# Expert jobs of 128 rows, with the second matrices of all experts resident in SBUF

## What is computed

```
logits = silu(x @ rw1 + rb1) @ rw2 + rb2          # 8 per token
k_logits, k_index = top_k(logits, 2);  k_prob = softmax(k_logits)
for e in range(8):
    we = sum(where(k_index == e, k_prob, 0))
    h  = silu(x @ w1[e] + b1[e]) @ w2[e] + b2[e]  # 128 -> 512 -> 128
    out += we * h
```

## Time and profile before

| | |
|---|---|
| median of three runs | 684.16 us |
| the profiled execution, its time | 685.29 us |
| its span, first to last instruction | 683.6 us |
| mean granted TensorE clock, share of full | 0.960 |
| attention and router, until the first job's up matmul | about 494 us |
| expert stage, first up to last down | about 494 to 655 us |
| reading back, weighting, residual | about 660 to 683 us |

### The profile page before, as it was taken

How to read it: one execution, slowest core, us unless ns; L and a number is a source line. 1 busy time by engine, 2 the same in 40 slices (tenths; PEclk the granted TensorE clock), 3 DMA queues, 4 the chain that set the end, 5 groups by cost and what they waited for, 6 DMA issues and landing times. The chain is left out here.

```text
span 683.6 us, 17706 instructions
## 1 busy us (share of the span) xinstructions
PE 588.5 (86%) x5108; PEld 439.8 (64%) x5108; DVE 507.1 (74%) x1888; ACT 508.8 (74%) x1578; POOL 423.3 (62%) x543
## 2 busy tenths in 40 slices
PE   5667789999899899899989989978798989999950
PEld 4444556666666566566666656655577979999940
DVE  6788988999999999999999999997565312222127
ACT  4157799999999999999989999998643434444434
POOL 2660655747668687686776966855366765554535
PEclk9777999999999999999999999999999999999975
DMA  5996678778787788778868878874525777565538
GB/s 142 308 230 202 198 235 248 228 235 248 214 245 241 213 252 246 228 219 260 249 208 242 252 213 247 243 236 148 189 82 174 236 234 228 198 217 185 176 97 274
DMA packets 173125, 149.03 MB, mean 218 GB/s; under 512 B 16182, under 2 KB 162642, under 8 KB 173030
## 3 DMA queue, kind: packets, MB, share of 16 engines
q1 hardware_dynamic: 168054, 139.33, 67.9%
q0 software_dynamic: 4544, 8.44, 3.7%
q10 hardware_dynamic: 432, 0.14, 0.1%
HBM read 83.71 MB, written 65.05 MB: 218 GB/s over the span
## 5 line engine op out<-in xcount | busy, mean ns | idle before, releaser
L711 ACT ACTIVATE P<-NS,nmax 128x256 f32<-128x256 f32 x512 | 254.2, 504 | 50.5 <-DVE nmax L1312 49.6
L1312 DVE CUSTOM_DVE_ANT_0 NS<-psS,bias 128x256 f32<-128x256 f32 x512 | 185.2, 417 | 2.3 <-PE psS L950 1.6
L968 PE MATMUL psT<-ident,P 128*128 128x128 f32 x1024 | 140.0, 281 | 8.9 <-ACT PT L722 8.8
L1267 DVE COPY stage<-psDist 128x768 f32<-128x768 f32 x125 | 118.1, 945 | 33.9 <-issue 25.2
L722 ACT ACTIVATE PT<-psT 128x512 f32<-128x512 f32 x256 | 136.4, 586 | 0.0
L968 PEld LDWEIGHTS psT<-ident,P 128*128 128x128 f32 x1024 | 118.2, 145 | 24.0 <-issue 9.8
L778 ACT ACTIVATE F<-psS,b1T 128x256 f32<-128x256 f32 x156 | 65.4, 471 | 86.5 <-PE psS L1061 86.5
L609 POOL DMA_INDIRECT results_d<-y,row_u x78 | 76.0, 974 | 56.7 <-DVE y L1458 40.8
L711 ACT ACTIVATION_READ_ACCUMULATOR P<-NS,nmax 128x1 f32 x512 | 100.3, 196 | 0.0
L950 PE MATMUL psS<-Kst,Qst 32*128 32x256 f32 x512 | 65.9, 336 | 34.7 <-DVE nmax L1312 29.9
L1061 PE MATMUL psS<-xT,w 128*128 128x256 f32 x312 | 80.6, 381 | 0.3 <-DMA w<-in_L_ffn_w_dram 0.3
(11 more groups left out here) (254 smaller groups left out, 1044.2 us busy)
## 6 DMA issues: line engine op xcount, KB each, us to landing
dist_d<-stage SPq DMA_DIRECT2D x128, 384.0 KB, 3.0
bias<-dist_d SPq DMA_DIRECT2D x256, 192.0 KB, 3.3
w<-in_L_ffn_w_dram SPq DMA_DIRECT2D x39, 512.0 KB, 3.7
x<-slots_d SPq DMA_DIRECT2D x39, 129.0 KB, 3.0
y<-results_d SPq DMA_DIRECT2D x16, 256.0 KB, 5.0
dist_d<-zeros SPq DMA_DIRECT2D x1, 2048.0 KB, 14.4
out_dram<-y SPq DMA_DIRECT2D x8, 256.0 KB, 3.2
results_d<-y,row_u POOLq DMA_INDIRECT x78, 3.0
```

The lines of the kernel that those rows point to most:

```text
L711: act.activation(P[:, p % 2, h, q, :], NS[:, p % 2, h, q, :], ACT.Exp, scale=-1.0, bias=nmax[:, p % 2, k:k + 1], accum_out=lsum[:, b % 2, ...
L968: mm = pe.transpose(psT[:, h, S * k + 128 * q:S * k + 128 * q + 128], P[:, p % 2, h, q, 128 * k:128 * k + 128], ident[:])
L1267: dve.tensor_copy(stage[:, p % STAGES, :, :, :], bank[:, :, 0:2 * RW].rearrange("p h (q c) -> p h q c", q=2)).then_inc(dist_out, 1)
L1312: dve.tensor_tensor_reduce(NS[:, p % 2, h, q, :], psS[:, h, S * q:S * q + S], bias[:, p, h, q, :], 1.0, 3e38, ALU.add, ALU.min, nmax[:, p ...
```

## The change

ET is 128, so a job has one tile; JOBS becomes 71 and FULL 41. The second matrices of all eight experts are loaded once, in attention, by eight DMAs on SP's queue (one per batch from batch 2 to 9) into `w2_s`, 16 KB per partition. `load_w` then loads the first matrix alone, 256 KB, into one of DEEP = 5 buffers, and waits for `up` where it waited for `down`. `go_down` takes its moving operand from `w2_s` at an address that depends on the expert's number, so PE needs that number in a register. PE, ACT and DVE load the numbers of four jobs at a time with the new function `of_tiles`; SP still loads one per job. A step of `tiles` is now a whole job: up of job n (four matmuls of 128 columns), the transpose for job n+1, down of job n-2. F has three buffers instead of two, `y` 24 instead of 12 (of half the size). The pads stand before jobs 33 and 37. `take_x` and `take_rows` are now done in every step. The steps that are interleaved with the closing of attention keep their numbers.

```diff
-ET = 256
+ET = 128
-HELD = 12
-DEEP = 4
-PADS = {FULL - 4: range(0, EXP // 2), FULL - 2: range(EXP // 2, EXP)}
+HELD = 24
+DEEP = 5
+PADS = {FULL - 8: range(0, EXP // 2), FULL - 4: range(EXP // 2, EXP)}
-        w = t("w", [128, DEEP, 2, HID])
+        w2_s = t("w2_s", [128, EXP, HID])
+        w1_s = t("w1_s", [128, DEEP, HID])
+        def of_tiles(engine_type, j, which):
+            if j % 4 == 0 or j == FULL:
+                last = min(j - j % 4 + 4, JOBS if j >= FULL else FULL)
+                _, which[j:last] = nc.values_load_multi_w_load_instructions(
+                    expert[0:1, j:last], engines=(engine_type,), min_val=0, max_val=EXP - 1)
+            return which[j]
...
+                    if n == 4 and 2 <= b < 2 + EXP:
+                        sp.dma_start(w2_s[:, b - 2, :], w2[:, b - 2, :]).then_inc(w2_in, 16)
...
             def load_w(j):
                 e = of_tile(sp, j)
-                past(sp, down, j + 1 - DEEP)
-                sp.dma_start(w[:, j % DEEP, :, :],
-                             w12[bass.ds(e, 1)].rearrange("a p s h -> p (a s) h")).then_inc(w_in[j % DEEP], 16)
+                past(sp, up, j + 1 - DEEP)
+                sp.dma_start(w1_s[:, j % DEEP, :],
+                             w1[bass.ds(e, 1)].rearrange("a p h -> p (a h)")).then_inc(w_in[j % DEEP], 16)
...
+            def unit(j):
+                if j == 0 or j == FULL:
+                    act.wait_ge(planned, 1 + j // FULL)
+                e = of_tiles(mybir.EngineType.Activation, j, which)
+                past(act, down, j - 2)
+                act.wait_ge(up, j + 1)
+                for k in range(HK):
+                    i = act.activation(F[:, j % 3, k, :], psH[:, j % 2, ET * k:ET * k + ET], ACT.Silu,
+                                       bias=b1T[:, bass.ds(e, 1), k:k + 1].rearrange("p a k -> p (a k)"))
...
+            def go_up(j):
+                pe.wait_ge(w_in[j % DEEP], arrivals(j))
+                pe.wait_ge(x_taken, j + 1)
+                past(pe, silu, j - 1)
+                past(pe, max_done, 4 * STEPS if j == 0 else 0)
+                for k in range(HK):
+                    mm = pe.matmul(psH[:, j % 2, ET * k:ET * k + ET], w1_s[:, j % DEEP, 128 * k:128 * k + 128],
+                                   xT[:, j % 2, :], start=True, stop=True)
...
+            def go_down(j):
+                if j == 0 or j == FULL:
+                    pe.wait_ge(planned, 1 + j // FULL)
+                past(pe, w2_in, 16 * EXP if j == 0 else 0)
+                e = of_tiles(mybir.EngineType.PE, j, which)
+                pe.wait_ge(silu, j + 1)
+                past(pe, y_rows, j - 1)
+                past(pe, ctx_done, B if j == 1 else 0)
                 for k in range(HK):
+                    mm = pe.matmul(psY[j % 2][:, 0:E], F[:, j % 3, k, :],
+                                   w2_s[:, bass.ds(e, 1), 128 * k:128 * k + 128].rearrange("p a e -> p (a e)"),
+                                   start=(k == 0), stop=(k == HK - 1))
...
             def tiles(first, last):
                 for n in range(first, last):
+                    if n < JOBS:
+                        go_up(n)
+                    if n + 1 < JOBS:
+                        turn_x(n + 1)
+                    if n > 1:
+                        go_down(n - 2)
...
             def take_rows(j):
                 dve.wait_ge(down, j + 1)
-                e = of_tile(dve, j)
+                e = of_tiles(mybir.EngineType.DVE, j, which)
                 past(dve, y_sent[j % HELD], 16 * EK * (j // HELD))
```

More of the change, by code:

```diff
@@ L168, in program @@
         attention(nc, block, sm, planned, x_v, X, ident, modT, mv, rstd, Wq, bq, Wk, bk, Wv, bv, Wo, bo, rel, c, wmod,
-                  ahead, rw1_s, rb1T, rw2_s, rb2T, w12, rows, slot_u, earlier, ones,
+                  ahead, rw1_s, rb1T, rw2_s, rb2T, w1, w2, rows, slot_u, earlier, ones,
                   slots_d, sent, p2, firstrow, expert, fill, filled, b1T, b2, out_v)
@@ L283, in attention @@
         jobno = t("jobno", [128, JOBS])
[L284 to L287, removed]
+        gone = t("gone", [128, MOST_JOBS, EXP])
+        gone_t = t("gone_t", [128, MOST_JOBS, EXP])
+        ex = t("ex", [128, MOST_JOBS])
+        first_f = t("first_f", [128, MOST_JOBS])
         used = t("used", [128, EXP + 1])
@@ L356, in attention @@
         b2_in = sm("b2_in")
+        w2_in = sm("w2_in")
         w_in = [sm(f"w_in{k}") for k in range(DEEP)]
@@ L661, in _ @@
             fill_rows(B - 2)
-            send_results(0, 1)
+            send_results(0, 2)
             send(B - 4)
             send(B - 3)
-            send_results(1, 3)
+            send_results(2, 6)
             fill_rows(B - 1)
@@ L765, in step @@
                     squash(b - 2, p - 6)
[L767 to L779, removed]
+            which = [None] * JOBS
+            def unit(j):
[7 more added lines that the diff above has]
+                                       bias=b1T[:, bass.ds(e, 1), k:k + 1].rearrange("p a k -> p (a k)"))
                 i.then_inc(silu, 1)
             def units(first, last):
-                for n in range(first, last):
-                    unit(n // 2, n % 2)
+                for j in range(first, last):
+                    unit(j)
             def weighted_part(c):
@@ L1048, in turn_x @@
                 past(pe, pt_done, 2 * STEPS if j == 0 else 0)
[L1049 to L1057, removed]
+                pe.transpose(psX[:, 0:128], x[:, j % DEEP, 0, 0:E], ident[:])\
+                    .then_inc(x_turned, 1)
@@ L1076, in tiles @@
+                mm.then_inc(down, 1)
             def tiles(first, last):
                 for n in range(first, last):
[L1078 to L1084, removed]
+                    if n < JOBS:
[4 more added lines that the diff above has]
+                        go_down(n - 2)
@@ L1139, in _ @@
             pe.matmul(psM[:, 0:EXP], ones[:], total[:], start=True, stop=True).then_inc(counted, 1)
-            tiles(11, 2 * GATES)
+            tiles(11, GATES)
             pe.wait_ge(planned, 2)
             pe.transpose(psM[0:B, 0:E], modT[:, 5, :], ident[:]).then_inc(gates_turned, 1)
-            tiles(2 * GATES, 2 * JOBS + 2)
+            tiles(GATES, JOBS + 2)
             pe.wait_ge(gates_out, 1)
-            pe.wait_ge(silu, 2 * JOBS)
+            pe.wait_ge(silu, JOBS)
             for b in range(B):
@@ L1448, in take_x @@
                     .then_inc(rows_known, 1)
-                past(dve, up, 2 * (j - 1))
+                past(dve, up, j - 1)
                 dve.tensor_copy(xT[:, j % 2, :], psX[:, 0:ET]).then_inc(x_taken, 1)
+            which = [None] * JOBS
             def take_rows(j):
@@ L1462, in tiles @@
                 for n in range(first, last):
[L1463 to L1467, removed]
+                    if n + 1 < JOBS:
+                        take_x(n + 1)
+                    if n > 1:
+                        take_rows(n - 2)
             def take_closing(n):
@@ L1593, in _ @@
             plan_rest()
-            tiles(13, 2 * JOBS + 2)
+            tiles(13, JOBS + 2)
             then(dve.tensor_tensor(vals[:], chosen[:], rep(logit[:], 1, 2), ALU.mult))
@@ L1659 @@
     inputs = dict(inputs)
-    w1, w2 = _np.asarray(inputs["L0_ffn_w1"]), _np.asarray(inputs["L0_ffn_w2"])
-    down = w2.reshape(EXP, HK, 128, E).transpose(0, 2, 1, 3).reshape(EXP, 128, HID)
-    inputs["L0_ffn_w12"] = _np.stack([w1, down], axis=2)
+    w2 = _np.asarray(inputs["L0_ffn_w2"])
+    inputs["L0_ffn_w2p"] = w2.reshape(EXP, HK, 128, E).transpose(2, 0, 1, 3).reshape(128, EXP, HID)
     for name in _INS:
```

22 lines of the change are left out of this document (7 added, 15 removed).

## The result

The changed kernel takes 709.06 us (median) where the kernel before takes 683.37 on the same chip: a ratio of 1.036, 95% interval 1.033 to 1.040. Slower was forecast, but 696 us with a range to 708. The forecast added 11.6 us to the profiled execution; it became 707.25 us (span 705.4).

The account below looks back on a forecast made before the run. SP's queue was to replace TensorE as the bound: w(16) at 527.6 + 122.6 of pairs + 9.8 of pads put w(70) at 660.0 and the last store at 669.9, +11.6 us, so 696 us; range 689 to 708.

Parts of the forecast that it names:

- step 11: Expert stage, after the steps interleaved with attention's closing: starts at 526.4 us, 2 us later than the present 524.42.
- SyncE's pair: SP's queue: issuing one job's x and w takes 2.27 us, more than TensorE's 1.90, so SP becomes the bound.
- the two pad groups: Eight pad DMAs on SP's queue: 5.25 + 4.5 = 9.8 us, counting in full once that queue is the bound.
- the early steps: Steps interleaved with attention's closing: 2 us later, bounds 0 and 5, from VectorE's added copies and register loads.
- TensorE's 1.90 us per job: TensorE in the expert stage: 0.90 up, 0.90 down and 0.105 transpose per 128-row job.
- w lands: Landing of a 256 KB first-matrix transfer: taken as 3.3 us, between x's 3.0 and w's 3.7.
- the loads of w2 in attention: Eight more 256 KB DMAs on SP's queue in attention: hidden, taken as 0; 9 us if each delayed a bias.
- From there SP doesn't wait any more: 54 pairs x 2.27 = 122.6: SP's queue after w(16) at 527.6 us: issues pairs without waiting, 122.6 us up to w(70) before adding the pads.
- The step on register loads: PE and DVE loading four expert numbers: TensorE's period 2.1 to 2.7 us; low end 2.15 taken, costing nothing under SP's.
- Rival 1: Register loads bound instead, above 2.27 us per job: 706 us at 2.5, 718 at 2.7; chance 0.15.
- Rival 2: SP doesn't bind and TensorE's saved columns show: 13 us faster, 671; chance 0.07 including mixtures near no change.
- Rival 3: Early stage slips 5 instead of 2 us, or attention feels the w2 loads (half of 9 us): 703; chance 0.08.

Follow-up runs that it names:

- the plan spread: Changed kernel with the 13 chained VectorE operations of plan_rest placed one behind each of steps 13 to 25 instead of all ahead of step 13; 703.8 us.
- fixed address: Changed kernel with the second matrix and its bias always of expert 0, so TensorE and VectorE load no expert numbers; 701.1 us.
- the queue alone freed: Changed kernel with SyncE loading its row and expert numbers four at a time; 705.2 us.
- with both: Changed kernel with expert 0 always for the second matrix and its bias, and SyncE loading row and expert numbers four at a time; 685.2 us.

## Why the prediction was wrong, step by step

| step of the sum | forecast | measured |
|---|---|---|
| step 11; w(16) issued | 526.4; 527.6 | 525.3; 526.7 |
| SyncE's pair, w(41) to w(70) | 2.27 | 2.32 |
| the two pad groups | 9.8 | 4.9 + 4.5 = 9.4 |
| waits at w(19) and w(20), for row numbers and `up` | 0 | 5.1 |
| w(16) to w(70), all told | 132.4 | 140.4 |
| w(70) issued | 660.0 | 667.1 |
| up(70) | 663.3 | 670.9 |
| last down, end of its issue | 666.9 | 677.0 |
| last row store | 669.9 | 679.5 |

w(70)'s 7.1 us are -0.9 at w(16), 5.1 of waiting, -0.4 of pads, and the rest, 3.3, the pairs: 54 x 0.06. Behind w(70) come 0.5 more to up(70), 2.5 more to the last down and -0.5 to the last row store: 9.6 us there in all.

**What held.** SyncE's queue became a bound at a beat near the forecast's, the pads cost what the rows said, the early steps slipped less than taken, TensorE's 1.90 us per job appears whenever nothing else holds it, w lands in 2.7 us (3.3 taken), and the loads of w2 in attention show no cost: step 0 comes at 492.3 us, 494.7 before. The 2.6 us that the prediction works out by the Trainium skill, "DMA: Bandwidth & Descriptors", its anatomy section, come near this, but the page gives that formula for DMAs that GpSimd issues, and these are SyncE's.

**What failed: the step "From there SP doesn't wait any more: 54 pairs x 2.27 = 122.6".** SyncE did wait, 5.1 us, a term that the sum put at nothing: 3.0 for the row numbers of job 14 and 2.1 for `up` of jobs 14 and 15, late because of `plan_rest` (next paragraph); with the plan spread these waits are gone. And the pairs were longer, 2.32 from w(41) on, which with shorter waits for row numbers (0.7 in all) makes the 3.3 us. The register loads of TensorE and VectorE are not the reason: without them (fixed address) w(16) to w(70) takes 140.4 us too, with 3.9 us of waiting at w(19) and pairs of 2.33.

**What was not in the sum: `plan_rest`.** It keeps its place in the text, ahead of step 13, and its length (4.2 us before, 4.7 now). But a step of 128 rows wants a new xT every time, where two half jobs of 256 shared one: the same block of work was covered before (rows above) and has no cover now. The forecast counted the copies' own time (2 us early on) and not what else stands in VectorE's queue between two of them. In the trace it costs TensorE 5.6 us (12.44 from step 13 to 16 where three take 6.8), 3.5 of it idle and most of the rest the lower clock that went with it; spread over 13 steps, it left a time of 703.8.

**The step on register loads**, "I take the low end, 2.15, which stays under SP's 2.27 and costs nothing", failed too, in another way than by the steady pace. Its own bounds were 2.1 to 2.7 us per job; it measured 2.26 to 2.28. That is SyncE's pace, so between w(16) and w(70) the loads cost nothing indeed, but they stand beside SyncE's queue as a second bound: with the queue alone freed, steps 0 to 70 are 2.5 us shorter, with both 20.9. What they cost in the changed kernel lies at the two ends. Without them steps 0 to 11 take 3.2 us less (the forecast had 2.5 us of loads in its early slip), and from w(70) to the end of the last down it is 6.4 us instead of 9.9, where the forecast had 6.9. The bounds of the parts were good: TensorE late by 0.3 to 1.5 (0.85 here), VectorE by 0.6 to 1.8 (0.65 here over two steps); together 1.4 to 1.5 us per four jobs, where the low end has 0.9. The error was the choice of the low end of both, where the trace had no row of a load on TensorE, and the cover, 0.9 us, is half of the 1.8 from the load to the matmul that needs it (625.2 to 626.97).

The loads in the tail: VectorE's last group (jobs 68 to 70) stands between down(68) and its y, which frees the bank that the last down needs (timeline, answering):

```profile
673.64 1.06 PE L1084 MATMUL psO<-w_s,F 128*128 x8
...
675.59 0.29 DVE L1472 TENSOR_TENSOR y<-psT,b2R 128x128 f32<-128x128 f32 x1 [4.06 <-PE psO L1084]
...
676.13 1.15 PE L1084 MATMUL psT<-w_s,F 128*128 x8 [1.44 <-DVE y L1472]
...
679.47 0.97 POOL L622 DMA_INDIRECT results_d<-y,row_u  x1 [0.30 <-issue]
```

**The rivals.** Rival 1 named the mechanism and a price that nearly fits (706 at 2.5 us per job), but its condition, TensorE's period above SyncE's, was not met: the test was "gaps that come every fourth job", and they do, while taking the loads away left the pace where it was (2.33), for SyncE holds it too. Rival 2 was right in its arithmetic, 671, though not for this kernel: a kernel took 671.2, with step 70 at 638.2 (638.5 in the rival), when SyncE's pair was 1.79, its pads gone, the plan spread and the loads covered. That step 11 came 2.1 us earlier there than the rival has it makes the match in part luck. Rival 3's early slip did not come.

## What to carry to other kernels

When a chain is replaced as the bound, list every chain whose period is within some 10% of the new one, and price each at its middle, not at its kinder end: two equal chains hide each other in one-at-a-time experiments (6.9 and 2.8 us alone, 22.8 together). A register load costs what is left of it when the matmuls queued ahead of it run out, so put it ahead of a wait that the engine has anyway, one value at a time (71 such loads were free here). When jobs are halved, look through each in-order queue for blocks of fixed length that sit between two of the now more frequent hand-overs.

## What was not expected of the hardware

- Of a group load of four numbers on TensorE, the load itself is 0.33 us; the four bounds checks with the gaps around them are 1.13. Loading four at once took only 0.24 us per value off SyncE (pair 2.27 to 1.79): of the load and the check of each value, the check stays, one per value.
- With an idle stretch of 3.5 us the granted clock fell to its lower level for 6.9 us, and matmuls ran at half speed; with idle gaps of 0.85 us every fourth job the clock stayed at its upper level throughout (600 to 672, 1.00).
- Landing was slower where the DMA engines were busier: 512 KB landed in 3.7 us with a DMA share of 0.65, and in 4.7 with 0.89 (256 KB in 2.7 with 0.58).
